# Slot attention of a four-stage block: weighted sums in quarters between the score quarters, queries scaled after their projection, the inverse root in two parts

## What is computed

```python
Pn = rmsnorm(P, input_norm_w); k = Pn @ Wk.T; v = Pn @ Wv.T      # P is ctx
for _ in range(3):
    sn = rmsnorm(slots, slot_norm_w)
    scores = einsum('bkd,bmd->bkm', sn @ Wq.T, k) * SCALE
    attn = softmax(scores, axis=-2)              # over the 56 slots
    attn = attn / (sum(attn, axis=-1) + EPS)     # over the 1500 rows
    slots = gru_cell(einsum('bkm,bmd->bkd', attn, v), slots)
```

## Time and profile before

| | us |
|---|---|
| median of 3 runs (lowest to highest) | 836.36 (835.56 to 839.57) |
| the profiled execution, own time | 839.22 |
| its span, first to last instruction | 837.4 |
| PE / DVE / ACT / POOL busy | 701.3 / 583.1 / 538.8 / 415.4 |
| slot attention, first scores to the last new slots | about 473.7 to 701.5 |

### The profile page before, as it was taken

The page is one execution under the profiler, slowest core; times in us unless marked ns, Lnnn a source line. Parts: engine busy times, 40 slices in busy tenths (PEclk is TensorE's granted clock), DMA queues, the critical chain, the costliest instruction groups (busy, mean ns, idle before and its releaser), DMA issues.

```text
span 837.4 us, 24107 instructions
## 1 busy us (share of the span) xinstructions
PE 701.3 (84%) x9015; PEld 501.7 (60%) x9015; DVE 583.1 (70%) x1077; ACT 538.8 (64%) x1167; POOL 415.4 (50%) x492
## 2 busy tenths in 40 slices
PE   5787999999999999948733668888887785899997
PEld 2255777777777777737411468777777783444543
DVE  5965888888888878834587567767767765566663
ACT  3355777777777777734372499877888983355554
POOL 1859677777777777400000033544444530366664
PEclk9789999999999999987875978899989997899999
DMA  6316444444444444240400504441442440212100
GB/s 196 103 43 174 144 131 130 128 128 128 128 128 128 128 130 136 56 85 2 181 1 1 228 2 154 154 153 58 174 155 77 155 153 0 76 39 73 43 0 23
DMA packets 26801, 86.41 MB, mean 103 GB/s; under 512 B 5780, under 2 KB 7316, under 8 KB 26724
## 3 DMA queue, kind: packets, MB, share of 16 engines
q1 hardware_dynamic: 26472, 85.03, 32.2%
q10 hardware_dynamic: 256, 0.40, 0.3%
HBM read 65.72 MB, written 0.46 MB: 79 GB/s over the span
## 4 chain that ended last, share of the span: by engine, by line
PE 54%; DVE 13%; POOL 12%; ACT 9%; issue 7%; DMA 2%; ACTq 1%; SPq 1%; POOLq 0%; DVEq 0%
PE ps L1311 8%; POOL ctx_lo L588 8%; PE ps L1328 8%; PE ps L1342 8%; PE ps L1567 5%; ACT c_prob L766 4%; PE ps L1298 4%; PE ps L1551 4%; PE ps L1287 2%; PE ps L1347 2%; ACT w0T L766 1%; ACTq L674 1%; DVE amax_part L1048 1%; PE ps L1585 1%; PE ps L1586 1%
## 5 line engine op out<-in xcount | busy, mean ns | idle before, releaser
L853 DVE TENSOR_REDUCE tile_max<-ps 128x1 f32<-128x500 f32 x336 | 215.1, 675 | 51.3 <-PE ps L1311 50.4
L614 ACT ACTIVATE probs<-ps 125x896 f32<-125x896 f32 x192 | 175.2, 916 | 108.0 <-PE ps L1328 95.7
L1311 PE MATMUL ps<-k_hi,qdiag 128*128 128x500 f16 x336 | 130.8, 392 | 6.9 <-DVE tile_max L853 5.7
L766 ACT ACTIVATE c_prob<-ps,c_bias,row_scale 125x56 f32<-125x56 f32 x384 | 116.4, 482 | 3.0 <-DVE c_bias L1134 2.7
L1328 PE MATMUL ps<-qstack,kstack 98*125 98x224 f16 x768 | 109.2, 266 | 0.4
L565 POOL TENSOR_TENSOR c_prob<-c_prob,c_weight 125x672 f32<-125x672 f32 x32 | 41.9, 1312 | 134.5 <-DVE c_weight L1148 134.5
L588 POOL TENSOR_TENSOR ctx_lo<-ctx_hi,ctx_lo 128x448 f16<-128x448 f32 x64 | 72.1, 1127 | 70.4 <-ACT ctx_lo L811 70.4
L1328 PEld LDWEIGHTS ps<-qstack,kstack 98*125 98x125 f16 x768 | 88.2, 140 | 21.3 <-ACT probs L614 3.3
L1342 PE MATMUL ps<-probs,v_aug 125*32 125x168 f32 x1536 | 76.9, 319 | 12.8 <-ACT probs L614 12.8
L1621 PE MATMUL ps<-ctx_lo 128*128 128x448 f16 x192 | 68.5, 357 | 6.7 <-DVE ctx_hi L1246 3.0
L521 POOL TENSOR_TENSOR rows_in<-rows_in 125x768 f32<-125x768 f32 (+2 forms) x96 | 68.8, 717 | 7.5
(11 more groups left out here) (251 smaller groups left out, 1699.3 us busy)
## 6 DMA issues: line engine op xcount, KB each, us to landing
row_tiles<-in_ctx_rows_wide SPq DMA_DIRECT2D x40, 774.0 KB, 5.7
ctx<-in_ctxT SPq DMA_DIRECT2D x16, 750.0 KB, 5.5
rows_in<-in_ctx_rows SPq DMA_DIRECT2D x16, 750.0 KB
kstack<-k_hi SPq DMA_DIRECT2D x128, 93.8 KB, 2.5
kstack<-k_lo SPq DMA_DIRECT2D x64, 93.8 KB, 2.6
ctx_hi<-in_wg SPq DMA_DIRECT2D x8, 256.0 KB, 2.7
ctx_hi<-in_wu SPq DMA_DIRECT2D x8, 256.0 KB, 3.0
ctx_hi<-in_wd SPq DMA_DIRECT2D x8, 256.0 KB, 3.6
```

What stands on the lines that cost most here:

```text
L614: nc.scalar.activation(probs[c % RING_P][0:CH, :].rearrange("p (k w) -> p k w", k=2), score_tile(c)[0:CH], ACT.Exp, scale=float(HD) ** -0. ...
L766: last = nc.scalar.activation(c_prob[n % PROBS][:, c, :], ps[0:CH, 2 * (n % 2) + c // 6, bass.ts(c % 6, TOK)], ACT.Exp, bias=c_bias[n % 2] ...
L853: nc.vector.reduce_max(tile_max[:, u % MAXT, u // MAXT:u // MAXT + 1], ps[:, MAXB + (u + p) % 2, 0:KCOLS], AX.X).then_inc(max_done, 1)
L1311: nc.tensor.matmul(ps[:, MAXB + (u + p) % 2, 0:KCOLS], qdiag[p][:, bass.ts(t, 128)], k_hi[p][:, bass.ts(j, KCOLS)], start=True, stop=True) ...
```

## The change

The weighted sums of each pair are cut into four pieces of three chunks (`update_sums(pair, k)`), one each in four successive slots: offsets 18 to 21 (behind the third and fourth quarter of A's scores and the first two of B's) and 26 to 29 (the same for C and D). The wait for the weighted probabilities stands before the first piece, the signal `u_ready` behind the last. The transposes move from offset 31 to 35, the new slots from 41 to 43 (behind the update's rows, before D's maxima), the copy of the updates from 28 to 31, the two gates' tanh from 36 to 37 (behind B's first three exponentials), the candidate from 39 to 40.

The means of the squares are now one matmul 128 x 224 against the full matrix of 1/128, so that each row holds them, and the projection of the raw slots follows at once (offset 51, behind A's scores). `spread_roots`, `normed_slots` and the separate `project_slots` are gone; DVE scales the projected slots in PSUM by the root (`scaled_queries`, offset 57), ACT's high half is at 57 and DVE's low half at 58. The root is 224 columns wide; on POOL it is one Newton step at offset 44 and one of higher order (six operations) at 48, ten operations in all. DVE's guess moves from 45 to 49. The unit's maxima `c_max` go to unused PSUM columns.

```diff
@@ -193,7 +193,7 @@
         query_lo = sbuf("query_lo", [128, T], F16, stack=sc)
-        c_max = [sbuf(f"c_max{i}", [CH, NCH], stack=sc) for i in range(2)]
+        c_max = [ps[0:CH, 2 * i, GW + 128:GW + 128 + NCH] for i in range(2)]
         c_bias = [sbuf(f"c_bias{i}", [CH, NCH], stack=sc) for i in range(2)]
@@ -303,10 +302,10 @@
-        TENSOR_AT = dict(spread=55, project=59, sums=(19, 27), turn=31, gates=39, means=47)
-        SCALAR_AT = dict(copy=28, tanh=36, cand=39, hi=54)
-        VECTOR_AT = dict(rows=27, hidden=39, slots=41, root=45, normed=53, lo=57)
-        POOL_AT = dict(root=40)
+        TENSOR_AT = dict(sums=(18, 26), turn=35, gates=39, means=51)
+        SCALAR_AT = dict(copy=31, tanh=37, cand=40, hi=57)
+        VECTOR_AT = dict(rows=27, hidden=39, slots=43, root=49, scaled=57, lo=58)
+        POOL_AT = dict(root=(44, 48))
@@ -568,17 +568,30 @@
                 pool.wait_ge(r_guess, g + 1)
-                for i in range(3):
-                    wait(pool, r_inv, 3 * g + i)
-                    nc.gpsimd.tensor_tensor(rs_a[:], rs_y[:], rs_y[:], ALU.mult).then_inc(r_step, 1)
-                    pool.wait_ge(r_step, 9 * g + 3 * i + 1)
-                    nc.gpsimd.tensor_tensor(rs_a[:], rs_a[:], rs_var[:], ALU.mult).then_inc(r_step, 1)
-                    pool.wait_ge(r_step, 9 * g + 3 * i + 2)
-                    nc.gpsimd.tensor_scalar(rs_a[:], rs_a[:], -0.5, 1.5, ALU.mult, ALU.add).then_inc(r_step, 1)
-                    pool.wait_ge(r_step, 9 * g + 3 * i + 3)
-                    nc.gpsimd.tensor_tensor(rs_y[:], rs_y[:], rs_a[:], ALU.mult).then_inc(r_inv, 1)
-            iterations(unit, [(POOL_AT["root"], True, inverse_root)])
+                nc.gpsimd.tensor_tensor(rs_a[:], rs_y[:], rs_y[:], ALU.mult).then_inc(r_step, 1)
+                pool.wait_ge(r_step, 8 * g + 1)
+                nc.gpsimd.tensor_tensor(rs_a[:], rs_a[:], rs_var[:], ALU.mult).then_inc(r_step, 1)
+                pool.wait_ge(r_step, 8 * g + 2)
+                nc.gpsimd.tensor_scalar(rs_a[:], rs_a[:], -0.5, 1.5, ALU.mult, ALU.add).then_inc(r_step, 1)
+                pool.wait_ge(r_step, 8 * g + 3)
+                nc.gpsimd.tensor_tensor(rs_y[:], rs_y[:], rs_a[:], ALU.mult).then_inc(r_inv, 1)
+            def second_root(g):
+                pool.wait_ge(r_inv, 2 * g + 1)
+                nc.gpsimd.tensor_tensor(rs_a[:], rs_y[:], rs_y[:], ALU.mult).then_inc(r_step, 1)
+                pool.wait_ge(r_step, 8 * g + 4)
+                nc.gpsimd.tensor_tensor(rs_var[:], rs_a[:], rs_var[:], ALU.mult).then_inc(r_step, 1)
+                pool.wait_ge(r_step, 8 * g + 5)
+                nc.gpsimd.tensor_scalar(rs_a[:], rs_var[:], 0.375, -1.25, ALU.mult, ALU.add).then_inc(r_step, 1)
+                pool.wait_ge(r_step, 8 * g + 6)
+                nc.gpsimd.tensor_tensor(rs_a[:], rs_a[:], rs_var[:], ALU.mult).then_inc(r_step, 1)
+                pool.wait_ge(r_step, 8 * g + 7)
+                nc.gpsimd.tensor_scalar(rs_a[:], rs_a[:], 1.875, None, ALU.add).then_inc(r_step, 1)
+                pool.wait_ge(r_step, 8 * g + 8)
+                nc.gpsimd.tensor_tensor(rs_y[:], rs_y[:], rs_a[:], ALU.mult).then_inc(r_inv, 1)
+            iterations(unit, [(POOL_AT["root"][0], True, inverse_root), (POOL_AT["root"][1], True, second_root)])
@@ -788,9 +801,8 @@
             def query_high(g):
-                act.wait_ge(qc_ready, g + 1)
-                nc.scalar.activation(query_hi[:, quad(g)], ps[:, QUERY, 288:288 + QT], ACT.Copy,
-                                     scale=norm_w[:, 1:2]).then_inc(qc_hi, 1)
+                act.wait_ge(r_slots, g + 1)
+                nc.scalar.activation(query_hi[:, quad(g)], projected, ACT.Copy, scale=norm_w[:, 1:2]).then_inc(qc_hi, 1)
@@ -1128,10 +1140,10 @@
                 wait(dve, c_biased, n - 1)
-                nc.vector.tensor_reduce(c_max[i][:].rearrange("p (k c) -> p k c", k=2), wide, AX.X, ALU.max).then_inc(c_maxed, 1)
+                nc.vector.tensor_reduce(c_max[i].rearrange("p (k c) -> p k c", k=2), wide, AX.X, ALU.max).then_inc(c_maxed, 1)
                 dve.wait_ge(c_maxed, n + 1)
                 wait(dve, c_exped, n - 1)
-                nc.vector.scalar_tensor_tensor(out=c_bias[i][:], in0=c_max[i][:], scalar=-1.0, in1=row_scale[:, n % BATCH, :],
+                nc.vector.scalar_tensor_tensor(out=c_bias[i][:], in0=c_max[i], scalar=-1.0, in1=row_scale[:, n % BATCH, :],
                                                op0=ALU.mult, op1=ALU.mult).then_inc(c_biased, 1)
@@ -1197,24 +1209,23 @@
                 dve.wait_ge(r_var, g + 1)
-                wait(dve, r_inv, 3 * g)
-                wait(dve, r_spread, g)
-                step(nc.vector.tensor_scalar(rs_var[:], ps[:, QUERY, 0:TOK], RMS_EPS, None, ALU.add), r_var_eps, g + 1)
+                wait(dve, r_inv, 2 * g)
+                wait(dve, r_slots, g)
+                step(nc.vector.tensor_scalar(rs_var[:], means, RMS_EPS, None, ALU.add), r_var_eps, g + 1)
                 nc.vector.tensor_scalar(rs_y[:].bitcast(I32), rs_var[:].bitcast(I32), -0.5, ROOT_GUESS, ALU.mult, ALU.add).then_inc(r_guess, 1)
-            def normed_slots(g):
-                dve.wait_ge(r_spread, g + 1)
-                wait(dve, qc_ready, g)
-                nc.vector.tensor_tensor(slots_n, slots_of(g), ps[:, QUERY, 64:64 + QT], ALU.mult).then_inc(r_slots, 1)
+            def scaled_queries(g):
+                dve.wait_ge(r_inv, 2 * g + 2)
+                nc.vector.tensor_tensor(projected, projected, rs_y[:], ALU.mult).then_inc(r_slots, 1)
 ...
                 dve.wait_ge(qc_hi, g + 1)
-                nc.vector.scalar_tensor_tensor(out=query_lo[:, quad(g)], in0=ps[:, QUERY, 288:288 + QT], scalar=norm_w[:, 1:2], in1=query_hi[:, quad(g)],
+                nc.vector.scalar_tensor_tensor(out=query_lo[:, quad(g)], in0=projected, scalar=norm_w[:, 1:2], in1=query_hi[:, quad(g)],
                                                op0=ALU.mult, op1=ALU.subtract).then_inc(qc_done, 1)
 ...
                 (VECTOR_AT["rows"], False, update_rows), (VECTOR_AT["hidden"], False, hidden_part), (VECTOR_AT["slots"], False, new_slots),
-                (VECTOR_AT["slots"], True, slot_squares), (VECTOR_AT["root"], True, root_guess), (VECTOR_AT["normed"], True, normed_slots),
+                (VECTOR_AT["slots"], True, slot_squares), (VECTOR_AT["root"], True, root_guess), (VECTOR_AT["scaled"], True, scaled_queries),
                 (VECTOR_AT["lo"], True, query_low)], before_drain=lambda: weights(UNITS_C - 1))
@@ -1554,20 +1565,23 @@
-            def update_sums(pair):
+            def update_sums(pair, k):
                 def sums(g):
                     m = 2 * g + pair
-                    pe.wait_ge(c_attended, 2 * m + 2)
-                    for n in (2 * m, 2 * m + 1):
-                        pe.wait_ge(rows_loaded[rows_of(n)], rows_landed(n))
-                    wait(pe, u_rows_done, g)
-                    for c in range(NCH):
+                    if k == 0:
+                        pe.wait_ge(c_attended, 2 * m + 2)
+                        for n in (2 * m, 2 * m + 1):
+                            pe.wait_ge(rows_loaded[rows_of(n)], rows_landed(n))
+                        wait(pe, u_rows_done, g)
+                    for c in range(NCH // SLOTS * k, NCH // SLOTS * (k + 1)):
                         for j in range(2):
 ...
                                                     start=(c == 0), stop=(c == NCH - 1), skip_group_check=True)
-                    last.then_inc(u_ready, 1)
+                    if k == SLOTS - 1:
+                        last.then_inc(u_ready, 1)
                 return sums
@@ -1590,26 +1604,12 @@
                 wait(pe, qc_done, g)
-                for i in range(QUAD):
-                    last = nc.tensor.matmul(ps[32 * i:32 * i + 32, QUERY, 0:TOK], ones_mean[:, 0:32], rms_sq[:, bass.ts(i, TOK)], start=True, stop=True)
-                last.then_inc(r_var, 1)
-            def spread_roots(g):
-                pe.wait_ge(r_inv, 3 * g + 3)
-                wait(pe, r_slots, g)
-                for i in range(QUAD):
-                    last = nc.tensor.matmul(ps[:, QUERY, 64 + TOK * i:64 + TOK * (i + 1)], spread[:, i, :], rs_y[:], start=True, stop=True)
-                last.then_inc(r_spread, 1)
-            def project_slots(g):
-                pe.wait_ge(r_slots, g + 1)
-                wait(pe, qc_done, g)
-                nc.tensor.matmul(ps[:, QUERY, 288:288 + QT], to_query[:], slots_n, start=True, stop=True).then_inc(qc_ready, 1)
+                nc.tensor.matmul(means, ones_mean[:], rms_sq, start=True, stop=True)
+                nc.tensor.matmul(projected, to_query[:], stream[:, quad(g)], start=True, stop=True).then_inc(r_var, 1)
             iterations(unit, [
-                (TENSOR_AT["spread"], True, spread_roots), (TENSOR_AT["project"], True, project_slots),
-                (TENSOR_AT["sums"][0], False, update_sums(0)), (TENSOR_AT["sums"][1], False, update_sums(1)),
```

(15 more changed lines are left out.)

## The result

The changed kernel takes 853.19 us (median of 4, 850.10 to 855.74) against 836.10 (median of 4, 835.56 to 839.57) for the kernel before, run beside it: ratio 1.016 (95% interval 1.012 to 1.020). It is slower, as forecast, by 17 us in the medians and by 10.9 in the two profiled executions (850.10 against 839.22). Run again later, beside the kernel before, it took 854.5 against 841.2, ratio 1.013 (1.004 to 1.021). Ratios and intervals leave out the executions more than 1.5% above the fastest of their kernel (three of "slots behind D's bias", one of the repeated changed kernel, whose median is 852.2 without it), while the medians given are of all.

The account below looks back on a forecast made before the run. It took a loop of waits across engines in the slot attention as the bound; +4.3 us at full clock and +5 us of clock loss, 9.3 in all on the median of 836.36, gave 845.5, range 833 to 853.

Parts of the forecast that it names:

- What decides: the pieces behind D: Slot attention: DVE's rows wait for piece four, two pieces sit between B's quarters; 18.4 to 18.5 a round against 17.3.
- The ninth round without query work: Slot attention's ninth round, without the squares: 18.1 in place of 15.93, +2.2 us.
- Before the first tanh: Start of the slot attention: DVE waits once for piece four, +1.0 us.
- The end: Last quad: D starts 1.3 later with its copy inside it, +1.7 us.
- The clock: PE's clock drops behind idle times: between 0 and 1.2 a round, middle taken, 0.6 a round, +5 us.
- The idle times of PE that I reasoned from: PE idle 1.5 before D's first quarter, 2.0 before A, 2.1 to 2.3 before B's first quarter.
- The sum: Whole kernel: +4.3 at full clock and +5 clock, 9.3 us on the median of 836.36, giving 845.5.
- Clock kept: Rival: pieces feed PE evenly, 2.4 GHz stays, DVE's chain slightly shorter; 836 to 840.5 us; chance 0.22.
- The old loop stays and is shorter: Rival: D's bias is ready in time, spreading's 0.92 leaves each round; 829, or 820 with full clock; chance 0.17.
- POOL: Rival: POOL's weighting of D slips behind the root's first part, delaying pieces one; 1.3 a round, 856; chance 0.06.
- The bias with its maxima in PSUM: DVE's bias with maxima in PSUM: perhaps a gain (0.17 median, 0.63 at worst), worth nothing to the sum.

Follow-up runs that it names:

- slots behind D's bias: Changed kernel with DVE's new slots and squares at offset 45 instead of 43, after D's maxima and bias: 837.6 us, ratio 0.995 to the kernel before.
- filled kernel: Changed kernel with throwaway matmuls in two of PE's idle times (48 behind D's scores, 60 behind the first pair's second piece): 846.2 us, ratio 1.006 to the kernel before.
- both pairs whole: Changed kernel with the sums of both pairs uncut again, at offsets 19 and 27: 837.9 us, ratio 0.998 to the kernel before.
- first pair whole: Changed kernel with only A and B's sums uncut, at offset 19, C and D's still in pieces: 835.8 us, ratio 0.994 to the kernel before.
- slots behind and both whole: Changed kernel with new slots at offset 45 and the sums of both pairs uncut: 836.9 us, ratio 0.995 to the kernel before.
- the two remedies: Changed kernel with new slots at offset 45 and A and B's sums uncut: 832.0 us, ratio 0.984; repeated 827.3, ratio 0.986 to the kernel before.
- only the second: Changed kernel with only C and D's sums uncut, at offset 27, A and B's still in pieces: 847.7 us, ratio 1.009 to the kernel before.

## Why the prediction was right

**The loop.** The step "What decides: the pieces behind D" gave 18.4 to 18.5 a round at full clock. Measured: 18.45, five times. The path and its waits stood where they were put: DVE's bias for D to ACT at 9.25 (9.3 said), ACT's wait before D 1.69 (1.6), the wait before the tanh 0.28 ("about half a us"). Two runs took each half of the cost away by itself, and a third both.

That the sum fits to the tenth is in part luck, for terms in it were off and cancelled. B's quarters and the two pieces, chain of waits, changed kernel:

```profile
582.38 0.41 PE ps L1562 x9
582.78 0.81 PE ps L1580 x12
583.59 0.34 PE ps L1562 x9
583.93 0.81 PE ps L1580 x12
584.74 0.57 PE ps L1562 x18
```

A piece takes 0.81 on the path where I had 0.66, so these are 2.93 and not 2.28, and piece four behind D ends at 5.85 and not 5.6. Against that DVE's rows need 0.73 (0.98 said), and D's exponentials with the copy and the hand-over 3.88 (4.3 said).

**The ninth round without query work.** 18.1 said; 18.17 in the filled kernel, where the clock stays, and 19.63 in the changed one, where a fall lies in it.

**Before the first tanh.** 1.0 said, 3.8 measured from the first scores on (41.28 against 37.50). This term was too small. In the filled kernel, where no fall lies just ahead of that tanh, it is 40.23; by that about 2.7 are order and 1.0 clock (the fall at 506.9 to 510.3). With both pairs whole it is 37.78: the pieces cost it, and they stand between the quarters of more than one unit before the first tanh.

**The end.** I had D's lateness and the copy, +1.7; at full clock it is 0.7. The tenth round came out even (14.52 against 14.74). What I missed stands in the last: the new slots of quad 10 are now behind the rows of quad 11 in DVE's queue, and the gates wait for both. Chain of waits, changed kernel:

```profile
702.69 0.17 DVE u_den L1175
...
703.98 0.40 DVE work L1200
...
704.93 1.09 PE ps L1599 x2
...
706.77 0.75 PE ps L1599 x2
```

The last round is 8.76 in the filled kernel against 7.81 before, so 0.95 is order; the other 1.7 of the changed kernel's 10.43 are the gates at half clock (0.75 for a pair that takes 0.38).

**The clock.** I took 0.6 a round, +5 in all, the middle between two ends that no row could narrow. That the eight rounds then lost exactly 0.6 on average is luck. Falls in the ninth round, in the last and before the first tanh added 1.5, 1.7 and 1.0: 9 in all. The idle times of PE that I reasoned from, 5.8 a round, measured 3.7 (0.82, 1.24 and 1.63). Nor does their sum decide: the run with the first pair whole has 3.1 a round and keeps the clock, the one with slots behind and both whole has 2.9 in one piece and loses it in every round.

**The sum.** Order came to 5.0 (-0.7, 2.2, 2.7, 0.7) where I had 4.3, clock to 9.0 where I had 5: 14.0 in the slot attention where 9.3 was forecast. The medians lie 17.1 apart; the 3 left over are within what the stages ahead, which the change does not touch, differ by from one execution to another. The profiled executions, 850.1 where 848.5 was forecast, came near for the same reason, since these stages were 2.8 shorter in the changed one. The median is 0.2 above the upper end of my range, and above the 850.5 that I gave as the forecast's own upper end (which, with 4.3 and 11 on 836.4, should have read 851.7). So path, direction and the loop's length were right, and the size was hit only at the edge of the range.

**Rivals.** "Clock kept" did not happen in the changed kernel and did in four variants of it (slots behind, first pair whole, both of these, filled). "The old loop stays and is shorter" is refuted by the loop's own waits; its time is near that of the two remedies (ratios 0.984 and 0.986 to the kernel before, where its 829 and 820 are 0.991 and 0.980), though a loop of another shape closes the round there. POOL: tested and refuted. What I did not see was that the same pieces do good behind D and harm between B's quarters.

**The bias with its maxima in PSUM**, by source line, changed kernel; it answers to the earlier trace rows:

```profile
L1146 DVE SCALAR_TENSOR_TENSOR c_bias<-ps,row_scale x48: 169/170/171, 473.0 to 692.9; 125x12 f32<-125x12 f32 x48
```

All 48 take 0.170, where before single ones took up to 0.632, although POOL does more. That is what the Trainium skill's rule on two SBUF inputs ("SBUF — State Buffer", "Who interferes with whom") would have, and the median is the same, so PSUM costs nothing. No run had the maxima in SBUF beside the wide root, so that the port is the cause is argued, not shown.

## What to carry to other kernels

Cutting a long block of matmuls into pieces between others moves the block's end later. Look for who waits for the last piece, and what is queued behind that waiting instruction on its own engine. Where an engine's list is written by hand, put the work whose result is due last behind the work that another engine is about to need; here one offset, 43 to 45, was worth 1.1 us a round with all sums in pieces, 0.5 with the first pair whole, and nothing with both whole. Compare a stage from its own first instruction, not from the start of the execution: here the stages ahead moved it by up to 11 us. Pieces belong where PE would stand idle, and not between quarters whose end is on the loop.

## What the runs showed of the hardware that was not expected

Idle times of PE of 0.82, 1.24 and 0.56 in a round left the clock at 2.4 GHz over eight rounds; a single one of 2.88 a round lowered it in each where both pairs were whole, and in seven of nine rounds where only the second was. 108 throwaway matmuls of 0.026 a quad in idle time made the slot attention 8 us shorter. A fall cost 1.5 to 1.7 where it landed on B's quarters and the gates, and about 1.4 on the last pieces of the second pair (20.5 against 19.11). In the changed kernel falls came in every second or third round, though the instructions and PE's idle times (0.82, 1.24, 1.63) are the same in nearly all.

On POOL, the step that only adds a constant (L590) takes twice as long as the one that multiplies and adds (L586), by source line:

```profile
L590 POOL TENSOR_SCALAR rs_a<-rs_a x8: 767/777/780, 530.8 to 664.9; 128x224 f32<-128x224 f32 x8
```

```profile
L586 POOL TENSOR_SCALAR rs_a<-rs_var 128x224 f32<-128x224 f32 x8 | 3.0, 378 | 0.7
```

I had put both at 0.4. Why the one is slower, the runs do not show. It cost nothing here, since POOL had the time.
